# Attention heads divided before the turn instead of after it, and V's bias added to the heads

## The chip, the core and the metric

The kernel runs on one core of a Trainium2 chip. The core has five engines that each run their own instruction stream in order: TensorE (PE, its weight loads PEld), VectorE (DVE), ScalarE (ACT), GpSimd (POOL) and SyncE (SP, which only issues DMAs). They are joined by semaphores. The metric is the device time of one execution in microseconds, and the median of several runs is compared.

## What is computed

A gated block: cross-attention from 8 x 512 tokens onto 8 x 1601 context rows (16 heads of 32), with 8-bit fake quantisation ahead of both projections, then a mixture of 32 experts with a shared expert.

```python
q = _qdq(x) @ _qdq(wq).T + bq
kv = cond @ wkv.T + bkv
k, v = jnp.split(kv, 2, axis=-1)          # heads of 32
attn = jax.nn.softmax(jnp.einsum('bnhd,bmhd->bhnm', q, k) * scale, axis=-1)
o = jnp.einsum('bhnm,bmhd->bnhd', attn, v).reshape(B, N, C)
out = _qdq(o) @ _qdq(wp).T + bp
...
x = x + jnp.tanh(g_xattn[0]) * xattn(_layernorm(x), ctx_2048, ...)
x = x + jnp.tanh(g_ffn[0]) * ffn(_layernorm(x), ...)
```

The softmax weights of a token sum to one, so adding V's bias to V before the weighted sum is the same as adding it to the divided head after it.

## The kernel before

Attention goes through 8 batches `b`, in each 4 groups `g` of 4 heads, in each 13 steps `kt` of 128 context rows: 416 steps, named by `steps()`. A step on TensorE computes the scores of four heads, transposed (`scores_of`, two PSUM banks `s_ps` in turn), ScalarE takes Exp of each into `probs` (`exp_of`), and a step later TensorE adds `probs` times V to the heads `o_ps` (`heads_of`). A score matmul waits for the Exp of two heads before it. The sums of the Exps go another way: GpSimd adds ten of the thirteen steps into `prob_acc`, and TensorE multiplies that and the other three steps by ones into `sum_ps` (`sums_of`, `accumulated_sums`). Each head's sum lies there repeated over its 32 rows.

Between the score matmuls of a group stands other work, as a list of tiles that all engines read from the same functions (`lead_tiles`, `fill_tiles`), and that share four PSUM banks `r_all` in turn (`Ring`). Each tile takes the next bank, and TensorE waits until the tile four places earlier has been drained. In a step, the list is spread over the four heads by its length. For the next group these tiles are: the query tile and two of four K pieces (step 0), two more K pieces (step 1), 64 `max` tiles (steps 3 to 11), from which VectorE takes the row maxima, and their turn. ScalarE and VectorE split each K piece into two fp16 parts, SyncE copies the parts into a stack for each head (L539), and the first max tile of a head waits for those DMAs. V tiles of the next batch stand in group 3 (steps 3 to 8) and group 0 (steps 1, 2, 4, 5, 7, 8, 10). VectorE drains them and adds V's bias on the way (L1259).

When a group is over, ScalarE copies the heads (`copy_heads`, L1070) and, once GpSimd's part is in, the sums (`copy_sums`, L1075). Later TensorE turns both, tokens into rows: tile `oT` (L773, four transposes) and tile `sumT` (L778, four fp32 matmuls with every 32nd column of the identity). VectorE inverts the turned sums, 16 a row (L1309), and multiplies (L1313) into `work`. Where the turn stands: step 2 of groups 2, 3 and 0 of the next batch, and step 10 of group 1 (`LATE_HEADS`).

Row work is spread over the steps too, and stands behind a step's tiles: `o_part` in group 0 (ScalarE's rounding behind steps 4 and 5, L973, its integers behind steps 7 and 8, L980), `h_part` in group 1 (VectorE's layernorm statistics behind step 0, L1193 and L1196, ScalarE's square root inside step 1, L960), `x_part` in group 2.

Of the kernel before, what the change touches and what calls it, by code (L numbers as in the profile page):

```python
# [26 lines left out]
P = 128  # L27
# [66 lines left out]
def head_tiles(b, g):  # L94
    return [("oT", b, g), ("sumT", b, g)]
# [138 lines left out]
def build(nc, x, ctx_in, g_xattn, g_ffn, wq, bq, wkv, bkv, wp, bp, gate_w, gate_bias, w1, w2, w3,  # L234
# [15 lines left out]
    with ctx:  # L250
# [69 lines left out]
        rsum = sb("rsum", [P, TT, GH], FP32)  # L320
# [127 lines left out]
        sums_copied = sem("sums_copied")  # L448
# [212 lines left out]
        def _(pe):  # L661
# [42 lines left out]
            def tile(key):  # L704
# [64 lines left out]
                elif kind == "oT":  # L769
                    pe.wait_ge(heads_copied, group(b, key[2]) + 1)  # L770
# [3 lines left out]
                elif kind == "sumT":  # L774
                    pe.wait_ge(sums_copied, group(b, key[2]) + 1)
                    ps = open_tile(*key)
                    for t in range(TT):
                        last = nc.tensor.matmul(ps[:, t * GH:(t + 1) * GH], sum_sb[:, t * P:(t + 1) * P],  # L778
                                                ident[:, ::DH], start=True, stop=True)
# [80 lines left out]
            def sums_of(s):  # L860

                kt = s % KT
                w, slot = rows(kt), s % HALVES
                if kt == FIRST_SUMS and s >= KT:
                    pe.wait_ge(sums_copied, s // KT)
                for j in range(GH):
                    last = nc.tensor.matmul(sum_ps[j * DH:(j + 1) * DH, :], ones[0:w, :], probs[0:w, slot, j, :],
                                            start=(kt == FIRST_SUMS), stop=False)
                last.then_inc(probs_used, 1)
# [71 lines left out]
        def _(act):  # L941
# [64 lines left out]
            def tile(key):  # L1006
# [8 lines left out]
                elif kind == "k":  # L1015
                    g, i = key[2:]
                    at, w = PIECE_AT[i], PIECE[i]
                    if i == 0 and group(b, g):

                        for j in range(GH):  # L1020
# [3 lines left out]
                                         bias=bk_col[:, g:g + 1]).then_inc(k_hi_ready, 1)  # L1024
                elif kind == "maxT":
# [41 lines left out]
            def copy_heads(n):  # L1067

                act.wait_ge(probs_used, (n + 1) * KT)
                nc.scalar.copy(oT_sb[:, :], o_ps[:, :]).then_inc(heads_copied, 1)  # L1070

            def copy_sums(n):

                act.wait_ge(acc_summed, n + 1)
                nc.scalar.copy(sum_sb[:, :], sum_ps[:, :]).then_inc(sums_copied, 1)  # L1075
# [7 lines left out]
            for b, g, kt in steps():  # L1083
                s = step_of(b, g, kt)
                fill = fill_tiles(b, g, kt)
                if kt == 0 and s:
                    copy_heads(s // KT - 1)
                for key in lead_tiles(b, g, kt):
                    tile(key)
                for j in range(GH):  # L1090
                    exp_of(s, j)
                    if j == 1 and g == 2 and b + 1 < B and kt == X_STD:
                        deviations(x_var_ready, b + 2, x_std_ready)
                    if j == 1 and g == 1 and b and kt == H_STD:
                        deviations(h_var_ready, b, h_std_ready)
                    for key in fill[len(fill) * j // GH:len(fill) * (j + 1) // GH]:
                        tile(key)
                if kt == 0 and s:
                    copy_sums(s // KT - 1)
                if g == 2 and b + 1 < B:  # L1100
                    x_part(b + 1, kt)
                if g == 0 and b:
                    o_part(b - 1, kt)
                if g == 1 and b:
                    h_part(b - 1, kt)
            copy_heads(B * GROUPS - 1)
            copy_sums(B * GROUPS - 1)
# [26 lines left out]
        def _(dve):  # L1134
# [110 lines left out]
            def tile(key):  # L1245
# [9 lines left out]
                elif kind == "v":  # L1255
                    t = key[2]
                    w = rows(t)
                    ps = full(dve, *key)
                    V.tensor_tensor(v_sb[0:w, t, :], ps[0:w, :], bv_row[0:w, :], ALU.add).then_inc(free_of(*key), 1)  # L1259
# [31 lines left out]
                elif kind == "sumT":  # L1291
# [11 lines left out]
            def heads_out(b, g):  # L1303

                if g == 0 and b:
                    dve.wait_ge(h_out, b * DMA)
                po = full(dve, "oT", b, g)
                pss = full(dve, "sumT", b, g)
                V.reciprocal(rsum[:, :, :].rearrange("p t j -> p (t j)"), pss[:, 0:TT * GH]  # L1309
                             ).then_inc(free_of("sumT", b, g), 1)  # L1310
                wait_read(dve, "sumT", b, g)
                for t in range(TT):
                    last = V.tensor_tensor(  # L1313
                        work[:, t, g * P:(g + 1) * P].rearrange("p (j d) -> p j d", j=GH),
                        po[:, t * P:(t + 1) * P].rearrange("p (j d) -> p j d", j=GH),
                        rsum[:, t, :].unsqueeze(2).to_broadcast([P, GH, DH]), ALU.mult)
                    if t < TT - 1:
                        step.mark(last)
                last.then_inc(free_of("oT", b, g), 1)
                wait_read(dve, "oT", b, g)  # L1320

# [4 lines left out]
            for b, g, kt in steps():  # L1326
                for key in lead_tiles(b, g, kt) + fill_tiles(b, g, kt):
                    tile(key)
                if g == 2 and b + 1 < B:
                    x_part(b + 1, kt)  # L1330
                if g == 0 and b:
                    o_part(b - 1, kt)
                if g == 1 and b:
                    h_part(b - 1, kt)
            heads_out(B - 1, GROUPS - 1)
# [313 lines left out]
```

## Time and profile before

| | us |
|---|---|
| median of three runs | 3153.32 |
| lowest, highest | 3148.29, 3154.59 |
| the profiled execution | 3147.53 |
| its span, first to last instruction | 3145.8 |
| one batch of attention | 300 |

The profile is one execution, taken by the hardware profiler. An idle time in it is given with the instruction that ended it (`<-`). "issue" is idle time for which the profile shows nothing. A wait on a weight load (PEld) is hidden in part by the matmul still running; the wait on the matmul itself (PE) is TensorE standing still. [...] Batches 1 to 7 repeat the same pattern to a few tenths of a microsecond.

### The profile page before, as it was taken

How to read it: one execution, taken by the hardware profiler on the slowest of the kernel's cores; microseconds unless marked ns; L12 is line 12 of the kernel's file. 1: busy time of each engine (PE TensorE's matmuls, PEld its weight loads, DVE VectorE, ACT ScalarE, POOL GpSimd, SP SyncE). 2: the span in 40 equal slices, each digit the busy share in tenths (PEclk: the TensorE clock that was granted, in tenths of full speed). 3: DMA queues.
4: the chain of work that ended last, by engine and by line, in shares of the span. 5: the costliest groups of instructions: out<-in, count | busy, mean ns of one | idle time of the engine just before them, and what ended most of it. 6: DMA issues, size and time to landing. Idle time of an engine off the chain costs nothing. (4 is left out here: it accounts for less than half of the span.)

```text
span 3145.8 us, 43433 instructions
## 1 busy us (share of the span) xinstructions
PE 2824.6 (90%) x14876; PEld 1215.4 (39%) x14876; DVE 1791.0 (57%) x3878; ACT 1383.7 (44%) x2460; POOL 1808.2 (57%) x1570
## 2 busy tenths in 40 slices
PE   5898999899989988999899899989998799998987
PEld 3333333333333333333333333333332354444766
DVE  6576567756675666667557756775664343433222
ACT  4155446644564456456545644564456210000111
POOL 0285567656656676667566656765668423223455
PEclk9798999999999999999999999999999899899999
DMA  4111012101211031103111201221011123131996
GB/s 126 39 45 52 24 35 72 54 22 35 77 53 39 18 94 47 35 22 95 30 35 58 66 23 35 72 54 33 23 53 57 68 99 110 61 121 55 310 282 116
DMA packets 146586, 215.59 MB, mean 69 GB/s; under 512 B 24984, under 2 KB 78232, under 8 KB 146368
## 3 DMA queue, kind: packets, MB, share of 16 engines
q1 hardware_dynamic: 130496, 195.95, 20.7%
q0 software_dynamic: 15872, 16.87, 2.9%
q8 instruction: 120, 1.97, 0.3%
q14 instruction: 98, 0.80, 0.1%
HBM read 126.49 MB, written 34.24 MB: 51 GB/s over the span
## 5 line engine op out<-in xcount | busy, mean ns | idle before, releaser
L1549 POOL TENSOR_TENSOR prob_acc<-prob_acc,probs 128x512 f32<-128x512 f32 x1152 | 1430.7, 1279 | 420.6 <-ACT probs L1065 420.6
L1065 ACT ACTIVATE probs<-s_ps 128x512 f32<-128x512 f32 (+1 forms) x1664 | 937.2, 596 | 770.0 <-PE s_ps L841 738.8
L1286 DVE TENSOR_REDUCE piece_max<-r_all 128x1 f32<-128x400 f32 (+1 forms) x2048 | 1027.7, 565 | 142.1 <-PE r_all L763 135.3
L763 PE MATMUL r_all<-k_flat,q_stack 96*128 96x400 f16 (+1 forms) x2048 | 604.7, 352 | 110.2 <-DVE piece_max L1286 41.4
L841 PE MATMUL s_ps<-q_stack,k_flat 97*128 97x512 f16 (+1 forms) x1664 | 631.1, 396 | 60.7 <-ACT probs L1065 52.5
L855 PE MATMUL o_ps<-probs,v_sb 128*32 128x512 f32 (+1 forms) x3328 | 465.3, 632 | 21.6 <-ACT probs L1065 21.6
L841 PEld LDWEIGHTS s_ps<-q_stack,k_flat 97*128 97x128 f16 (+1 forms) x1664 | 160.1, 101 | 630.5 <-ACT probs L1065 424.5
L1546 POOL COPY prob_acc<-probs 128x512 f32<-128x512 f32 x128 | 73.0, 616 | 494.1 <-PE sum_ps L875 359.5
L763 PEld LDWEIGHTS r_all<-k_flat,q_stack 96*128 96x128 f16 x2048 | 203.7, 100 | 387.7 <-DVE piece_max L1286 125.8
L1581 POOL DMA_INDIRECT slot_rows<-payload,slot x128 | 125.7, 982 | 300.1 <-DVE slot L1462 230.7
L1280 DVE SCALAR_TENSOR_TENSOR k_lo<-r_all,bk_col,k_hi 128x400 f16<-128x400 f32 (+1 forms) x128 | 81.7, 638 | 280.7 <-ACT k_hi L1023 280.7
L810 PE MATMUL r_all<-probs,k_flat 128*128 128x512 f32 x512 | 225.6, 599 | 0.9 <-DVE sum_sb L1424 0.9
L1259 DVE TENSOR_TENSOR v_sb<-r_all,bv_row 128x512 f32<-128x512 f32 (+1 forms) x104 | 71.8, 690 | 170.4 <-PE r_all L724 170.4
L1023 ACT ACTIVATE k_hi<-r_all,bk_col 128x400 f16<-128x400 f32 (+1 forms) x128 | 76.5, 598 | 182.5 <-PE r_all L753 182.5
L1608 POOL DMA_INDIRECT out_rows<-probs,slot_init x64 | 99.8, 1559 | 87.7 <-DMA out_rows<-probs,slot_init 52.2
L810 PEld LDWEIGHTS r_all<-probs,k_flat 128*128 128x128 f32 x512 | 97.5, 192 | 120.7 <-issue 119.7
L1054 ACT ACTIVATE oT_sb<-r_all 128x512 f32<-128x512 f32 x32 | 19.1, 597 | 259.7 <-PE r_all L810 243.9
L828 PE MATMUL r_all<-k_flat,probs 128*128 128x512 f32 x256 | 130.0, 667 | 1.5 <-DVE probs L1429 0.9
L855 PEld LDWEIGHTS o_ps<-probs,v_sb 128*32 128x32 f32 (+1 forms) x3328 | 66.7, 109 | 130.4 <-issue 70.8
L724 PE MATMUL r_all<-wkv_hi,ctx_hi 128*128 128x512 f16 (+1 forms) x416 | 112.8, 395 | 3.4 <-DVE ctx_lo L1252 1.8
L753 PE MATMUL r_all<-ctx_hi,wkv_hi 128*128 128x400 f16 (+1 forms) x512 | 109.6, 336 | 0.0
L724 PE MATMUL r_all<-wkv_hi,ctx_lo 128*128 128x512 f16 (+1 forms) x416 | 108.8, 385 | 0.0
(220 smaller groups left out, 2832.3 us busy)
## 6 DMA issues: line engine op xcount, KB each, us to landing
k_flat<-k_hi SPq DMA_DIRECT2D x256, 100.1 KB, 2.2
ctx_raw<-in_ctx SPq DMA_DIRECT2D x96, 256.0 KB, 2.8
xin<-in_x SPq DMA_DIRECT2D x16, 1024.0 KB, 5.6
k_flat<-k_lo SPq DMA_DIRECT2D x128, 100.1 KB, 2.2
v_sb<-in_L_ffn_w SPq DMA_DIRECT2D x18, 512.0 KB
q_stack<-q_hi SPq DMA_DIRECT2D x256, 32.0 KB, 1.8
h_rows<-work SPq DMA_DIRECT2D x8, 1024.0 KB, 4.5
x_rows<-xin SPq DMA_DIRECT2D x8, 1024.0 KB, 6.8
```

The source lines that it names most:

```text
L724: last = nc.tensor.matmul(ps[0:w, :], a[:, c, t * P:t * P + w], wt[:, 1, c, :], start=(n == 0), stop=(n == 3 * DC - 1))
L753: last = nc.tensor.matmul(ps[:, 0:w], wt[:, 0, c, g * P:(g + 1) * P], a[:, c, at:at + w], start=(n == 0), stop=(n == 3 * DC - 1))
L763: last = nc.tensor.matmul(ps[:, 0:w], q_stack[0:KSPLIT, g % 2, j, qt * P:(qt + 1) * P], k_stack[0:KSPLIT, g % 2, j, at:at + w], start=True ...
L810: last = nc.tensor.matmul(ps[:, :], wt[:, c, f * P:(f + 1) * P], hT[:, c, :], start=(c == 0), stop=(c == DC - 1))
L828: last = nc.tensor.matmul(ps[:, :], actT[:, f, t * P:(t + 1) * P], sd[:, f, :], start=(f == 0), stop=(f == FSC - 1))
L841: nc.tensor.matmul(s_ps[j % SBANKS][0:w, :], k_stack[:, g % 2, j, kt * P:kt * P + w], q_stack[:, g % 2, j, :], start=True, stop=True).then ...
L855: last = nc.tensor.matmul(o_ps[j * DH:(j + 1) * DH, :], v_sb[0:w, kt, h * DH:(h + 1) * DH], probs[0:w, slot, j, :], start=(kt == 0), stop= ...
L1065: nc.scalar.activation(probs[0:w, slot, j, :], s_ps[j % SBANKS][0:w, :], ACT.Exp).then_inc(probs_ready, 1)
L1286: V.reduce_max(piece_max[:, j * TT + qt, i:i + 1], ps[:, 0:PIECE[i]], X_AXIS).then_inc(free_of(*key), 1)
L1549: last = G.tensor_tensor(prob_acc[:, j, :], prob_acc[:, j, :], probs[:, slot, j, :], ALU.add)
L1581: G.indirect_dma_start(out=slot_scr, out_offset=bass.IndirectOffsetOnAxis(ap=slot[:, t, k:k + 1], axis=0), in_=payload[:, t, k, :], in_off ...
L1608: G.indirect_dma_start(out=out, out_offset=bass.IndirectOffsetOnAxis(ap=e_slots[:, e, 0:1].bitcast(I32), axis=0), in_=e_y[e % 2][:, h * HA ...
```

## The change

ScalarE no longer copies the sums, and TensorE no longer turns them. Instead VectorE, behind its tiles of step 0 of the next group, waits for the sums, inverts all of `sum_ps` into `sum_sb` (128x512) and multiplies the copied heads by it in place (`divide_heads`). The turn of the heads waits for that. What is turned is then already divided: VectorE adds V's bias to it in one operation on its way into `work` (`heads_out`). V tiles leave PSUM as plain copies on ScalarE. `copy_heads` now waits for the turn of the group before, which reads the buffer it writes.

```diff
 def head_tiles(b, g):
-    return [("oT", b, g), ("sumT", b, g)]
+    return [("oT", b, g)]
...
                 elif kind == "oT":
-                    pe.wait_ge(heads_copied, group(b, key[2]) + 1)
+                    pe.wait_ge(heads_divided, group(b, key[2]) + 1)
...
-                elif kind == "sumT":
-                    pe.wait_ge(sums_copied, group(b, key[2]) + 1)
-                    ps = open_tile(*key)
-                    for t in range(TT):
-                        last = nc.tensor.matmul(ps[:, t * GH:(t + 1) * GH], sum_sb[:, t * P:(t + 1) * P],
-                                                ident[:, ::DH], start=True, stop=True)
...
                 if kt == FIRST_SUMS and s >= KT:
-                    pe.wait_ge(sums_copied, s // KT)
+                    pe.wait_ge(sums_inverted, s // KT)
...
+                elif kind == "v":
+                    t = key[2]
+                    w = rows(t)
+                    ps = full(act, *key)
+                    nc.scalar.copy(v_sb[0:w, t, :], ps[0:w, :]).then_inc(free_of(*key), 1)
...
                 act.wait_ge(probs_used, (n + 1) * KT)
+                if n:
+                    act.wait_ge(bank_full[ring.last_bank("oT", (n - 1) // GROUPS, (n - 1) % GROUPS)],
+                                ring.done("oT", (n - 1) // GROUPS, (n - 1) % GROUPS))
                 nc.scalar.copy(oT_sb[:, :], o_ps[:, :]).then_inc(heads_copied, 1)
-
-            def copy_sums(n):
-
-                act.wait_ge(acc_summed, n + 1)
-                nc.scalar.copy(sum_sb[:, :], sum_ps[:, :]).then_inc(sums_copied, 1)
...
-                    V.tensor_tensor(v_sb[0:w, t, :], ps[0:w, :], bv_row[0:w, :], ALU.add).then_inc(free_of(*key), 1)
...
-                V.reciprocal(rsum[:, :, :].rearrange("p t j -> p (t j)"), pss[:, 0:TT * GH]
-                             ).then_inc(free_of("sumT", b, g), 1)
...
+                V.tensor_tensor(work[:, :, g * P:(g + 1) * P], po[:, :].rearrange("p (t n) -> p t n", t=TT),
+                                bv_row[:, g * P:(g + 1) * P].unsqueeze(1).to_broadcast([P, TT, P]), ALU.add
+                                ).then_inc(free_of("oT", b, g), 1)
                 wait_read(dve, "oT", b, g)
+
+            def divide_heads(n):
+
+                dve.wait_ge(acc_summed, n + 1)
+                V.reciprocal(sum_sb[:, :], sum_ps[:, :]).then_inc(sums_inverted, 1)
+                dve.wait_ge(sums_inverted, n + 1)
+                dve.wait_ge(heads_copied, n + 1)
+                V.tensor_tensor(oT_sb[:, :], oT_sb[:, :], sum_sb[:, :], ALU.mult).then_inc(heads_divided, 1)
...
+                if kt == 0 and s:
+                    divide_heads(s // KT - 1)
                 if g == 2 and b + 1 < B:
                     x_part(b + 1, kt)
```

The order on the engines shows three places; `r_all` is the shared PSUM, `probs` the Exps, `x4` four instructions in a row. First VectorE at the start of group 1 of batch 1, before:

```order
L1280 SCALAR_TENSOR_TENSOR k_lo<-r_all,bk_col,k_hi 128x401
L1280 SCALAR_TENSOR_TENSOR k_lo<-r_all,bk_col,k_hi 128x400
L1193 BN_STATS stats<-xin 128x6 x4
L1196 BN_AGGR mv<-stats 128x2 x4
L1280 SCALAR_TENSOR_TENSOR k_lo<-r_all,bk_col,k_hi 128x400 x2
```

and the same place now:

```order
L1269 SCALAR_TENSOR_TENSOR k_lo<-r_all,bk_col,k_hi 128x401
L1269 SCALAR_TENSOR_TENSOR k_lo<-r_all,bk_col,k_hi 128x400
L1305 RECIPROCAL sum_sb<-sum_ps 128x512
L1308 TENSOR_TENSOR oT_sb<-oT_sb,sum_sb 128x512
L1187 BN_STATS stats<-xin 128x6 x4
L1190 BN_AGGR mv<-stats 128x2 x4
L1269 SCALAR_TENSOR_TENSOR k_lo<-r_all,bk_col,k_hi 128x400 x2
```

The reciprocal and the product stand ahead of the statistics and of K's pieces 2 and 3. Next ScalarE in group 0 of batch 1, steps 1 to 8, before:

```order
L1023 ACTIVATE k_hi<-r_all,bk_col 128x400
L1065 ACTIVATE probs<-s_ps 128x512 x13
L973 ACTIVATE work<-work,rounder,inv 128x512 x2
L1065 ACTIVATE probs<-s_ps 128x512 x4
L973 ACTIVATE work<-work,rounder,inv 128x512 x2
L1065 ACTIVATE probs<-s_ps 128x512 x8
L980 ACTIVATE q_int<-work,rounder 128x512 x2
```

and now:

```order
L1064 ACTIVATE probs<-s_ps 128x512 x10
L1023 COPY v_sb<-r_all 128x512
L967 ACTIVATE work<-work,rounder,inv 128x512 x2
L1064 ACTIVATE probs<-s_ps 128x512 x4
L1023 COPY v_sb<-r_all 128x512
L967 ACTIVATE work<-work,rounder,inv 128x512 x2
L1064 ACTIVATE probs<-s_ps 128x512 x8
L1023 COPY v_sb<-r_all 128x512
L974 ACTIVATE q_int<-work,rounder 128x512 x2
```

A copy of V stands directly ahead of each pair of rounding and integer operations. Last TensorE in group 1 of batch 0, at the turn behind step 10's max tiles, before:

```order
L773 MATMUL r_all<-ident,oT_sb 128x128 x4
L778 MATMUL r_all<-ident,sum_sb 128x4 x4
L841 MATMUL s_ps<-q_stack,k_flat 128x512
L763 MATMUL r_all<-k_flat,q_stack 128x401
L763 MATMUL r_all<-k_flat,q_stack 128x400
```

and now:

```order
L773 MATMUL r_all<-ident,oT_sb 128x128 x4
L835 MATMUL s_ps<-q_stack,k_flat 128x512
L763 MATMUL r_all<-k_flat,q_stack 128x401
L763 MATMUL r_all<-k_flat,q_stack 128x400
```

The four matmuls of the sum tile are gone from between the turn and the next step.

## Rows read from the trace of the kernel before

**Rows 1.** The page, part 1: busy us (share of span), instructions, by engine

```profile
PE 2824.6 (90%) x14876; PEld 1215.4 (39%) x14876; DVE 1791.0 (57%) x3878; ACT 1383.7 (44%) x2460; POOL 1808.2 (57%) x1570
```

**Rows 2.** Line L763, the max tiles: whom TensorE waited for, us, times

```profile
  DVE work L1313: 24.0, 30
...
  DVE v_sb L1259: 14.7, 51
```

**Rows 3.** Groups by line: operation, shapes, count | busy us, mean ns | idle before

```profile
L1070 ACT COPY oT_sb<-o_ps 128x512 f32<-128x512 f32 x32 | 18.8, 586 | 65.1 <-PE sum_ps L867 65.1
...
L1309 DVE RECIPROCAL rsum<-r_all 128x16 f32<-128x16 f32 x32 | 8.0, 250 | 92.1 <-PE r_all L778 92.1
...
L1144 DVE RECIPROCAL inv<-so 128x4 f32<-128x4 f32 x8 | 1.4, 178 | 0.3
L1462 DVE TENSOR_TENSOR slot<-slotf,over 128x16 int32<-128x16 f32 x8 | 1.4, 175 | 0.3
```

**Rows 4.** Timeline, batch 4, group 0, steps 2 and 3: start, duration, instruction [idle before]

```profile
1325.98 1.08 PEld L778 LDWEIGHTS r_all<-ident,sum_sb 128*128 128x128 f32 x8
...
1327.55 0.88 DVE L1313 TENSOR_TENSOR work<-r_all,rsum 128x128 f32<-128x128 f32 x4
...
1328.48 0.34 PE L763 MATMUL r_all<-k_flat,q_stack 96*128 96x400 f16 x1 [0.54 <-DVE work L1313]
```

**Rows 5.** Timeline, step 3 of group 3 (batch 3) and of group 2 (batch 4)

```profile
1250.63 0.52 PE L763 MATMUL r_all<-k_flat,q_stack 96*128 96x401 f16 x2 [1.34 <-DMA k_flat<-k_hi]
...
1470.31 0.61 PE L841 MATMUL s_ps<-q_stack,k_flat 97*128 97x512 f16 x1 [2.31 <-ACT probs L1065]
```

**Rows 6.** Timeline, batch 4, group 0, around the ends of steps 4 and 7

```profile
1337.77 1.51 ACT L973 ACTIVATE work<-work,rounder,inv 128x512 f32<-128x512 f32 x2
...
1341.70 0.69 DVE L1259 TENSOR_TENSOR v_sb<-r_all,bv_row 128x512 f32<-128x512 f32 x1 [2.81 <-PE r_all L724]
...
1341.99 1.14 ACT L1065 ACTIVATE probs<-s_ps 128x512 f32<-128x512 f32 x2 [2.72 <-PE s_ps L841]
...
1343.71 0.10 PEld L841 LDWEIGHTS s_ps<-q_stack,k_flat 97*128 97x128 f16 x1 [0.84 <-ACT probs L1065]
...
1357.08 1.32 ACT L980 ACTIVATE q_int<-work,rounder 128x512 bf16<-128x512 f32 x2
...
1359.83 0.69 DVE L1259 TENSOR_TENSOR v_sb<-r_all,bv_row 128x512 f32<-128x512 f32 x1 [1.49 <-PE r_all L724]
...
1361.84 0.10 PEld L841 LDWEIGHTS s_ps<-q_stack,k_flat 97*128 97x128 f16 x1 [0.84 <-ACT probs L1065]
```

**Rows 7.** Timeline, VectorE at K's piece 2, step 1 of batch 3's group 3

```profile
1242.96 0.64 DVE L1280 SCALAR_TENSOR_TENSOR k_lo<-r_all,bk_col,k_hi 128x400 f16<-128x400 f32 x1 [4.99 <-ACT k_hi L1023]
```

**Rows 8.** Timeline, batch 4, group 1, steps 0 to 3

```profile
1395.47 2.46 DVE L1193 BATCH_NORM_STATS2 stats<-xin 128x6 f32<-128x512 f32 x4
...
1397.37 0.59 ACT L1075 COPY sum_sb<-sum_ps 128x512 f32<-128x512 f32 x1 [0.37 <-PE sum_ps L875]
...
1397.97 0.38 DVE L1196 BATCH_NORM_AGGREGATE mv<-stats 128x2 f32<-128x6 f32 x4
...
1400.25 0.30 ACT L960 ACTIVATE std<-mv,eps 128x4 f32<-128x4 f32 x1
...
1403.22 0.10 PEld L841 LDWEIGHTS s_ps<-q_stack,k_flat 97*128 97x128 f16 x1 [0.17 <-ACT probs L1065]
...
1408.29 0.34 PE L763 MATMUL r_all<-k_flat,q_stack 96*128 96x401 f16 x1 [1.80 <-DMA k_flat<-k_hi]
```

**Rows 9.** Windows: us; busy of PE, PEld, DVE, ACT, POOL; clock; DMA share, GB/s

```profile
1408.30:1412.30 4.00, 4.00 (x16) 0.96 (x17) 1.63 (x3) 0.72 (x2) 4.00 (x4) 0.57 0.67 156
```

**Rows 10.** Timeline, the end of attention

```profile
2457.04 1.12 PE L773 MATMUL r_all<-ident,oT_sb 128*128 128x128 f32 x4
...
2457.17 0.59 ACT L1075 COPY sum_sb<-sum_ps 128x512 f32<-128x512 f32 x1 [7.64 <-PE sum_ps L875]
...
2459.54 3.65 PE L797 MATMUL r_all<-ident,ctx_lo 128*128 128x128 f32 x16
```

More of the change, by code:

```diff
@@ L319, in build @@
         prob_acc = sb("prob_acc", [P, GH, N], FP32)
-        rsum = sb("rsum", [P, TT, GH], FP32)
         hT, actT = probs[:, 0], probs[:, 1]
@@ L447, in build @@
         heads_copied = sem("heads_copied")
-        sums_copied = sem("sums_copied")
+        sums_inverted = sem("sums_inverted")
+        heads_divided = sem("heads_divided")
         h_ready = sem("h_ready")
@@ L1097, in _ @@
                         tile(key)
-                if kt == 0 and s:
-                    copy_sums(s // KT - 1)
                 if g == 2 and b + 1 < B:
@@ L1106, in _ @@
             copy_heads(B * GROUPS - 1)
-            copy_sums(B * GROUPS - 1)
             for key in [("hT", 0, c) for c in range(DC)] + [("logits", 0)]:
@@ L1254, in tile @@
                                     ctx_hi[:, :, t * P:t * P + w], ALU.subtract).then_inc(free_of(*key), 1)
[L1255 to L1258, printed above, removed]
-                    V.tensor_tensor(v_sb[0:w, t, :], ps[0:w, :], bv_row[0:w, :], ALU.add).then_inc(free_of(*key), 1)
                 elif kind == "q":
@@ L1290, in tile @@
                         V.reduce_max(row_max[:, :], piece_max[:, :, :], X_AXIS).then_inc(row_max_ready, 1)
-                elif kind == "sumT":
+                elif kind == "oT":
                     heads_out(b, key[2])
@@ L1307, in heads_out @@
                 po = full(dve, "oT", b, g)
-                pss = full(dve, "sumT", b, g)
-                V.reciprocal(rsum[:, :, :].rearrange("p t j -> p (t j)"), pss[:, 0:TT * GH]
-                             ).then_inc(free_of("sumT", b, g), 1)
[L1311 to L1319, printed above, removed]
-                wait_read(dve, "oT", b, g)
+                V.tensor_tensor(work[:, :, g * P:(g + 1) * P], po[:, :].rearrange("p (t n) -> p t n", t=TT),
+                                bv_row[:, g * P:(g + 1) * P].unsqueeze(1).to_broadcast([P, TT, P]), ALU.add
+                                ).then_inc(free_of("oT", b, g), 1)
+                wait_read(dve, "oT", b, g)
+            def divide_heads(n):
[4 more added lines that the diff above has]
+                V.tensor_tensor(oT_sb[:, :], oT_sb[:, :], sum_sb[:, :], ALU.mult).then_inc(heads_divided, 1)
             for key in first_tiles():
@@ L1326, in _ @@
             for b, g, kt in steps():
+                s = step_of(b, g, kt)
                 for key in lead_tiles(b, g, kt) + fill_tiles(b, g, kt):
                     tile(key)
+                if kt == 0 and s:
+                    divide_heads(s // KT - 1)
                 if g == 2 and b + 1 < B:
@@ L1334, in _ @@
                     h_part(b - 1, kt)
+            divide_heads(B * GROUPS - 1)
             heads_out(B - 1, GROUPS - 1)
```

## The prediction

> **What bounds the kernel now.** I read the page first: TensorE is busy for 90% of the span, VectorE and GpSimd for 57%, ScalarE for 44% [rows 1]. A change elsewhere moves the end only if it moves a moment at which TensorE starts something. So I next read whom TensorE waits for ahead of its max tiles (L763): for the head tile's drain on VectorE (L1313) 24.0 us, for the V tile's drain on VectorE (L1259) 14.7 us [rows 2]. The 24.0 us count each wait twice, once for the weight load and once for the matmul, so 30 entries are 15 places. The durations come from the view by lines [rows 3], and the places from the timeline of one batch, which repeats every 300 us.
>
> **The sum tile goes away.** Its four fp32 matmuls keep TensorE's queue for 1.08 us [rows 4], and the head tile ahead of it is drained only once both are turned: the max tile that needs its bank stood still for 0.54 us more. There are 32 head tiles, and they stand in five kinds of place.
> - In group 0 at step 2 (7 batches) and in group 1 at step 10 (8 batches) nothing else waits: these are the 15 places above. Of 1.08 us about 0.95 is time that nothing else used, and with 0.54 us the gain is 1.5 us each, 15 x 1.5 = 22 us. The drain itself falls from 0.25 + 0.88 us [rows 3, 4] to one 128x512 addition, 0.69 us [rows 6], so I expect no wait in its place.
> - In group 2 at step 2 (8 places) TensorE waits 2.31 us for the Exp behind the square root, and in group 3 at step 2 (8 places) 1.34 us for the K stack [rows 5]. The wait grows by what the sum tile leaves: gain 0. If that cover went, each would be worth 1 us.
> - At the end of attention (1 place) it is counted below.
>
> **V leaves PSUM by ScalarE.** 104 tiles move. VectorE's add of 0.69 us ends the wait of 14.7 us, a copy takes 0.586 us [rows 2, 3, 6], so a bank comes free 0.1 us earlier: 51 waits x 0.1 = 5 us, with 0 and 14.7 as bounds. On ScalarE the copy stands behind the step's last Exp and ahead of the next step's first. In group 3 that time is idle. In group 0 it is not: at steps 4, 5, 7 and 8 ScalarE rounds the quantised heads (1.51 us) or turns them into integers (1.32 us), and did so while TensorE computed V. Now these instructions are queued behind a copy that waits for V to be complete. At step 4, V is complete at 1341.70; copy 0.59, rounding 1.51: the first Exp of step 5 starts at 1343.8 instead of 1341.99 and ends at 1344.4, and the third score matmul, which ran at 1343.71, waits for it: 0.75 us. At step 7: complete 1359.83, + 0.59 + 1.32 = 1361.75, Exp to 1362.35, against a score matmul at 1361.84: 0.55 us [rows 6]. Step 8 gives 0.1 by the same working, step 5 nothing, since the sum matmuls over step 4 lie between. That is 1.4 us x 7 batches = 10 us lost; the bounds are 5 (half of it finds slack) and 20 (0.75 at each of four steps).
>
> **The division ahead of the turn.** VectorE now waits for the group's sums, inverts 128x512 from PSUM, and multiplies 128x512. The trace has no reciprocal of this size. A reciprocal of 4 columns takes 178 ns and one of 16 takes 250 ns: 6.0 ns a column, so 512 columns take 0.178 + 508 x 0.0060 = 3.2 us. An addition takes 175 ns for 16 columns [rows 3] and 0.69 us for 512 [rows 6], 1.04 ns a column. Bounds: 0.69 us, if a long reciprocal streams like the addition and the 250 ns are a short instruction's overhead, and 6.2 us, if half of the 12 columns between the two hid in it (12 ns a column). I take 3.2, as the two rows are the same instruction, and 2.5 to 4.2 as near it. [...]
>
> Where does the wait stand? At step 0 of each group, ahead of K's pieces 2 and 3 on VectorE. In groups 0, 2 and 3 VectorE was idle for 4.99 us there [rows 7]; with 3.2 + 0.7 us K's piece 2 is drained about 1 us late and piece 3, which starts the stack's DMAs, on time. That costs nothing as long as the reciprocal is under 5 us.
>
> In group 1 (7 batches) the statistics of the next layernorm (2.46 + 0.38 us) stood in that idle time and were done before the sums came. Now they are queued behind the division, and ScalarE's square root, in the middle of step 1, waits for them, and with it K's piece 2, the Exp table and all later Exps. From [rows 8]: sums complete 1397.37, + 3.2 + 0.07 (semaphore) + 0.69 + 0.07, then 2.88 for the statistics: 1404.3, against the square root at 1400.25. The delay is R + 0.83 with R the reciprocal, so 4.0 us. TensorE has no slack there: its first score matmul of step 2 already waited 0.17 us for an Exp, and K's piece 3 on ScalarE comes after those Exps, so the DMA that TensorE awaits at 1408.29 moves by the same 4.0 us. 7 x 4.0 = 28 us lost.
>
> A second price there is the clock. [...] Another wait of 4 us comes now. [...] I take 0 and keep 12 for the range.
>
> **The end of attention.** The turn of the last heads went ahead at 2457.04, without the sums; now it waits for the division, from 2457.17 to 2461.2, then takes 1.1 us, and the 16 transposes of the next stage, at 2459.54 [rows 10], start at 2462.3: 2.8 us lost. The first stage and everything past it don't change.
>
> **Sum:** -22 - 5 + 10 + 28 + 2.8 = +14 us. The profiled execution took 3147.5 us (span 3145.8 and 1.7 around it) and would take 3161; the median of the three runs is 5.8 us above it, and from there I predict 3167 us, 0.4% slower than that median.
>
> **Rivals.**
> 1. The reciprocal streams. R = 0.69: group 1 loses 7 x 1.5 = 10.6 us, the end 0.3, and the sum is -22 - 5 + 10 + 10.6 + 0.3 = -6, 3147 us: faster. It decides from R under 1.5 us, where the sum crosses zero (8R - 12). Against it: six adds' worth a column in both short ones. For it: only short ones are seen, and a short instruction's fixed part may hold it all. [...] 0.12.
> 2. The clock falls a second time in group 1 after the longer wait: +12 on my sum, 3179 us. For it: one short wait did it. Against: the two waits are parted by work, and a slow stretch between them hides in the second. 0.14.
> 3. The change takes the sum tile from TensorE but the gain doesn't arrive, as the turned tile, now one place later in its step, is waited for as before: +22, 3189 us. Against it: nothing but VectorE's drain was late there, and it gets shorter. 0.06.
> 4. ScalarE's and group 1's delays are partly made up by slack that I don't see (half of 38 us): -5, 3148 us. Against it: TensorE's waits there end on exactly these rows. 0.09.
> 5. The reciprocal takes over 5 us. At 6.2 group 1 loses 21 more, the end 3, and K's piece 3 is 1.2 us late in the other 24 places, 29 us: +67, 3220 us. For it: nothing longer than 16 columns was seen. Against it: the two rows. 0.05.
>
> **How the numbers follow.** My case holds 0.54, from 3157 to 3180 by R from 2.5 to 4.2 and the bounds on V. A measurement of this kernel tells 0.2% (6.3 us) from no change. Range: from 3149, which leaves out most of rival 1, to 3184, which takes in rival 2. Faster 0.11 (most of rival 1), same 0.18 (rival 4, the rest of 1, and the low edge of my case), slower 0.71.
>
> **What would show it.** Right: the reciprocal of 128x512 near 3.2 us; the square root in group 1 four microseconds later behind the statistics, with TensorE idle for them at step 2; the wait on L1313's successor near 0; the Exp after rounding in group 0 at 1.8 us later, with a wait of the third score matmul. Wrong: a reciprocal near 0.7 us or over 5 us (then K's piece 3 is late in every group), or waits for the head tile's division ahead of the turn.

## The result and the profile after

| | before | changed |
|---|---|---|
| median of six runs, us | 3150.81 | 3177.34 |
| lowest, highest, us | 3142.89, 3158.37 | 3167.34, 3180.49 |
| profiled execution (span), us | 3147.53 (3145.8) | 3177.9 (3176.1) |

The ratio is 1.008 (95% interval 1.0059 to 1.0102): slower, as forecast and within the range, but by 26.5 us where the sum said 14. That is four times the 0.2% that the prediction took as the least that can be told.

The page of the changed kernel, part 1 (answers [rows 1]) and two groups of part 5, the new reciprocal and V's copies (operation, shapes, count | busy us, mean ns | idle before):

```profile
PE 2814.8 (89%) x14580; PEld 1192.5 (38%) x14620; DVE 1856.0 (58%) x3710; ACT 1419.9 (45%) x2532; POOL 1823.7 (57%) x1570
...
L1305 DVE RECIPROCAL sum_sb<-sum_ps 128x512 f32<-128x512 f32 x32 | 107.5, 3358 | 105.0 <-PE sum_ps L869 105.0
...
L1023 ACT COPY v_sb<-r_all 128x512 f32<-128x512 f32 (+1 forms) x104 | 61.0, 586 | 223.4 <-PE r_all L724 223.4
```

TensorE has 10 us less to do, and the profiled execution takes 30 us longer. The reciprocal takes 3.36 us. Whom the max tiles of L763 waited for, with the weight loads, us and times, in the changed kernel (answers [rows 2]):

```profile
  ACT v_sb L1023: 9.3, 51
  DVE work L1297: 6.1, 16
```

The two waits that the change was to shorten are shorter: 24.0 us became 6.1, and 14.7 became 9.3. What grew is seen in the view of waits on TensorE itself (us in total, times, longest us), for the score matmuls and the K stack. Before:

```profile
PE s_ps L841 <- ACT probs L1065: 52.5, 66, 2.3
...
PE r_all L763 <- DMA k_flat<-k_hi: 34.1, 17, 3.4
```

The same two rows in the changed kernel:

```profile
PE s_ps L835 <- ACT probs L1064: 89.2, 85, 3.7
...
PE r_all L763 <- DMA k_flat<-k_hi: 24.7, 17, 3.6
```

36.7 us more for Exps, 9.4 us less for the K stack. The timeline of batch 4, group 1, shows where (answers [rows 8]; start, duration, instruction [idle before]):

```profile
1400.83 1.06 PE L869 MATMUL sum_ps<-prob_acc,ones 128*32 128x512 f32 x8
...
1401.96 3.36 DVE L1305 RECIPROCAL sum_sb<-sum_ps 128x512 f32<-128x512 f32 x1 [1.81 <-PE sum_ps L869]
...
1405.36 0.84 DVE L1308 TENSOR_TENSOR oT_sb<-oT_sb,sum_sb 128x512 f32<-128x512 f32 x1
...
1406.12 2.46 DVE L1187 BATCH_NORM_STATS2 stats<-xin 128x6 f32<-128x512 f32 x4
...
1409.03 0.30 ACT L954 ACTIVATE std<-mv,eps 128x4 f32<-128x4 f32 x1 [4.30 <-DVE mv L1190]
...
1411.78 1.10 PE L835 MATMUL s_ps<-q_stack,k_flat 97*128 97x512 f16 x2 [3.73 <-ACT probs L1064]
...
1416.84 0.34 PE L763 MATMUL r_all<-k_flat,q_stack 96*128 96x401 f16 x1 [0.50 <-DMA k_flat<-k_hi]
```

The square root stood still for 4.30 us behind the statistics, TensorE for 3.73 us behind the Exps. From the accumulated sums to the first max tile it is 1416.84 - 1400.83 = 16.01 us; before it was 12.06 (its sums start at 1396.23, the max tile at 1408.29 [rows 8]).

The end of attention, timeline of the changed kernel (answers [rows 10]):

```profile
2471.68 1.94 PE L869 MATMUL sum_ps<-prob_acc,ones 128*32 128x512 f32 x8 [6.30 <-POOL prob_acc L1541]
...
2477.89 1.11 PE L773 MATMUL r_all<-ident,oT_sb 128*128 128x128 f32 x4 [4.28 <-DVE oT_sb L1308]
...
2478.80 3.62 PE L791 MATMUL r_all<-ident,ctx_lo 128*128 128x128 f32 x16
...
2483.30 7.01 PE L798 MATMUL r_all<-gateT,probs 128*128 128x32 f32 x32 [0.88 <-ACT probs L1040]
```

Sums to transposes: 7.12 us, 4.37 before, and 7.01 us for 32 router matmuls that took 4.62 before.

**The stages.** The window from the first accumulated sums to the last, before (us; busy of PE, PEld, DVE, ACT, POOL; TensorE's granted clock as a share of full speed; DMA share, GB/s):

```profile
198.60:2455.17 2256.57, 2053.71 (x11527) 778.76 (x11526) 1429.69 (x2815) 1229.98 (x2184) 1490.08 (x1269) 0.96 0.17 47
```

And in the changed kernel:

```profile
198.71:2471.68 2272.97, 2037.62 (x11243) 748.95 (x11279) 1499.41 (x2662) 1259.60 (x2244) 1506.07 (x1269) 0.95 0.17 47
```

Attention takes 16.4 us more. Divided at each start of accumulated sums, the seven spans of group 0 take 6.3 us more in all, the eight of group 1 10.3 more, group 2 0.9 less, group 3 0.8 more. The router stage behind it (up to the first bias of the shared expert) takes 22.1 us instead of 17.0. That is 21.5 us in the stages that the change touches. Another 9 us of the two traces' difference lie in the shared expert, whose code is the same. Its window before:

```profile
2472.18:2920.70 448.52, 412.63 (x1292) 209.73 (x1291) 171.61 (x717) 48.46 (x85) 132.99 (x146) 0.91 0.26 86
```

and after:

```profile
2493.80:2951.80 458.00, 420.56 (x1291) 216.32 (x1291) 171.64 (x717) 48.58 (x85) 132.50 (x146) 0.90 0.25 84
```

The same matmuls were busy 8 us longer at a slightly lower granted clock (0.90 against 0.91). In these traces the clock is at one of two levels: in windows of half a microsecond over batch 4's group 1 of before it is 1.00 up to 1408.5 us, 0.50 from 1409.0 to 1411.5 and 1.00 again from 1412.0 on.

### The profile page after: what moved, and what is told of

It reads as the page before. It is cut to its first block and busy times, and to the rows that moved or that the text cites. A ratio compares the mean times of both kernels' runs of the same rounds, so it can differ in the third digit from the quotient of the medians.

```text
span 3176.1 us, 42792 instructions
## 1 busy us (share of the span) xinstructions
PE 2814.8 (89%) x14580; PEld 1192.5 (38%) x14620; DVE 1856.0 (58%) x3710; ACT 1419.9 (45%) x2532; POOL 1823.7 (57%) x1570
## 5 line engine op out<-in xcount | busy, mean ns | idle before, releaser
L1541 POOL TENSOR_TENSOR prob_acc<-prob_acc,probs 128x512 f32<-128x512 f32 x1152 | 1446.6, 1290 | 435.6 <-ACT probs L1064 435.5
L763 PE MATMUL r_all<-k_flat,q_stack 96*128 96x400 f16 (+1 forms) x2048 | 604.6, 352 | 95.8 <-DVE piece_max L1275 45.2
L763 PEld LDWEIGHTS r_all<-k_flat,q_stack 96*128 96x128 f16 x2048 | 204.2, 100 | 369.0 <-DVE piece_max L1275 130.1
L1305 DVE RECIPROCAL sum_sb<-sum_ps 128x512 f32<-128x512 f32 x32 | 107.5, 3358 | 105.0 <-PE sum_ps L869 105.0
L1023 ACT COPY v_sb<-r_all 128x512 f32<-128x512 f32 (+1 forms) x104 | 61.0, 586 | 223.4 <-PE r_all L724 223.4
```

What stands on the lines that cost most here:

```text
L763: last = nc.tensor.matmul(ps[:, 0:w], q_stack[0:KSPLIT, g % 2, j, qt * P:(qt + 1) * P], k_stack[0:KSPLIT, g % 2, j, at:at + w], start=True ...
L1305: V.reciprocal(sum_sb[:, :], sum_ps[:, :]).then_inc(sums_inverted, 1)
L1541: last = G.tensor_tensor(prob_acc[:, j, :], prob_acc[:, j, :], probs[:, slot, j, :], ALU.add)
```

## The experiments

They ran in three sets (e1 to e4, e5 to e8, e9 and e10) on three chips, where the kernel before has medians of 3099.3, 3098.8 and 3098.7 us instead of 3151, so evidently not on the chip of the pair above. Ratios are compared, each to the runs of before in its own set, and traces of these runs with each other. First the pair once more. "Before again" is the kernel before, "after again" the changed kernel.

> The kernel before once more, for a second trace. The stretch after attention is within 3 us of the first trace's if the clock's phase there is fixed by the program; if it is chance, it differs by as much as the two traces of the changed kernel do.

> The changed kernel once more, for a second trace. If the stretch after attention, which the change does not touch, really got longer, it is again 9 to 13 us longer than in the trace of before; if that is the clock's phase in one execution, it differs from the first trace by several us.

The results of all, with the attention (first accumulated sums to last) and the router stage of the profiled execution, and the mean length of group 0 and 1 in batches 1 to 6:

| kernel | ratio to before (95%) | attention | router | group 0 | group 1 |
|---|---|---|---|---|---|
| before again | 1 | 2257.5 | 17.0 | 84.6 | 61.2 |
| after again | 1.0074 (1.0050 to 1.0098) | 2276.0 | 19.9 | 85.2 | 62.4 |
| e1, statistics first | 0.9996 (0.9973 to 1.0019) | 2247.4 | 19.4 | 85.0 | 58.5 |
| e2, V copies only | 1.0016 (1.0000 to 1.0033) | 2246.6 | 17.2 | 85.8 | 59.7 |
| e3, division only | 1.0042 (1.0029 to 1.0056) | 2262.4 | 20.0 | 83.5 | 63.6 |
| e5, rows ahead of V | 1.0075 (1.0050 to 1.0099) | 2273.5 | 20.0 | 83.4 | 63.6 |
| e6, turn behind transposes | 1.0088 (1.0060 to 1.0116) | 2274.1 | 15.4 | 84.9 | 62.7 |
| e7, e1 + e5 + e6 | 0.9944 (0.9923 to 0.9965) | 2230.0 | 13.9 | 83.5 | 59.3 |
| e9, e1 + e5 | 0.9950 (0.9927 to 0.9973) | 2230.7 | 19.9 | 83.2 | 59.4 |
| e10, e3 + e1 + e6 | 0.9918 (0.9894 to 0.9943) | 2237.2 | 13.9 | 83.2 | 59.7 |

The pair repeats: attention and router stage together are 21.4 us longer here (18.5 + 2.9), 21.5 on the first chip. Place by place they differ: group 0 is 5.6 us longer (6.3 on the first chip), group 1 7.0 (10.3), and groups 2 and 3 together 6.0, which on the first chip were 0.1 shorter. The shared expert's stage is 4 us shorter after than before, with the clock at 0.97 and 0.98, and what follows it 6 us longer (228.1 against 221.8, on the first chip 224.3 against 225.1). The code of both is the same, so nothing shows that the 9 us in the first pair of traces come from the change. Group 0 of the changed kernel swings alike on both chips: 86.6 to 86.7, 84.8, 84.8, 83.3 to 83.4, 88.0, 83.4, 86.7 for batches 1 to 7, where before it held within 0.7 us. It swings with the granted clock. Windows over the group in batches 1, 3 and 4, changed kernel, first chip (columns as in [rows 9]):

```profile
410.21:496.95 86.74, 80.06 (x425) 29.79 (x426) 54.88 (x91) 43.10 (x78) 53.28 (x44) 0.96 0.08 20
...
1015.25:1100.07 84.82, 78.19 (x425) 29.32 (x426) 54.88 (x91) 43.09 (x78) 53.28 (x44) 0.98 0.08 20
...
1317.47:1400.83 83.36, 76.67 (x424) 28.94 (x425) 54.88 (x91) 42.81 (x78) 53.30 (x44) 1.00 0.09 20
```

The two groups of 83.4 us have 1.00, the two of 84.8 have 0.98, and the three of 86.7 and more have 0.96. All groups 0 of before have 0.98. Batch 5, the longest, has 1.2 us more besides, at one place in its last third that these runs leave unexplained.

### e1: the statistics of group 1 ahead of the division

```diff
+                if g == 1 and b:
+                    h_part(b - 1, kt)
                 if kt == 0 and s:
                     divide_heads(s // KT - 1)
...
-                if g == 1 and b:
-                    h_part(b - 1, kt)
```

> The changed kernel, but in group 1 VectorE runs the layernorm statistics ahead of the division, as it ran them ahead of the sums before. Theory 1 (the statistics queued behind the division hold ScalarE's square root, and TensorE 3.7 us, in 7 batches): the wait of the step-2 score matmul in group 1 is back near 0.2 us, each group 1 of batches 1 to 7 is 2 to 4 us shorter than in the changed kernel (61.8 to 63.8 us there, sums to sums), so 59 us, a little under the 60.5 of before for the missing sum tile; in all 15 to 28 us under the changed kernel, 3150 to 3162 us. Rival (V's copies and the clock carry the loss): within 5 us of the changed kernel, 3172 or more.

The ratio falls from 1.0074 to 0.9996, some 24 us and within the 15 to 28 expected, and the attention by 28.7. Batch 4, group 1, timeline of e1:

```profile
1393.17 1.06 PE L869 MATMUL sum_ps<-prob_acc,ones 128*32 128x512 f32 x8
...
1395.20 3.33 DVE L1305 RECIPROCAL sum_sb<-sum_ps 128x512 f32<-128x512 f32 x1
...
1397.08 0.30 ACT L954 ACTIVATE std<-mv,eps 128x4 f32<-128x4 f32 x1
...
1405.22 0.34 PE L763 MATMUL r_all<-k_flat,q_stack 96*128 96x401 f16 x1 [1.79 <-DMA k_flat<-k_hi]
```

The reciprocal takes as long as ever (3.33 us against 3.36), but stands behind the statistics. The square root waits for nothing, and from sums to max tile it is 12.05 us, the 12.06 of before. So the price of group 1 was not the reciprocal but what was queued behind it.

### e2 and e3: each half alone

e2 is the kernel before with V drained by copies on ScalarE; V's bias is left out of its computation. e3 is the changed kernel with V drained and biased by VectorE as before, and the turned heads only copied.

```diff
+                    nc.scalar.copy(v_sb[0:w, t, :], ps[0:w, :]).then_inc(free_of(*key), 1)
...
-                    V.tensor_tensor(v_sb[0:w, t, :], ps[0:w, :], bv_row[0:w, :], ALU.add).then_inc(free_of(*key), 1)
```

> The kernel before, but ScalarE copies V out of PSUM; V's bias is left out of the computation altogether. Sum tile, division and turn are as before. Theory 1 (a copy ahead of ScalarE's rounding and integers in group 0 delays the next Exps): group 0 of batches 1 to 7 about 1.4 us longer (84.5 before), group 3 unchanged, 5 to 10 us over before in all, 3156 to 3161 us. Rival (VectorE relieved of 0.69 us per V tile, banks free earlier): 5 to 10 us under before.

> The changed kernel, but VectorE drains V with its bias added, as before, and the turned heads are only copied into the rows. Theory 1: the division alone costs 28 us in group 1 and 5 at the end, its missing sum tile gives 22 back and the clock some: 5 to 15 us over before, and with the V copies' part the measured 26 of the whole. Rival (division harmless, V's move carries the loss): within 3 us of before or faster.

By medians V's copies cost 5 us (by the interval hardly to be told from none), the division 13 to 15, the two 18 to 20 of the 23 to 26 of the whole. V's copies make group 0 1.2 us longer, with the clock at 0.98 in all batches as before. The division makes it 1.1 us shorter, and 0.8 in the six batches that are at 0.98 (83.7 against 84.5 and 84.6): that is the sum tile's gain. Each half alone is steady, e3 at 83.6 to 83.9 in six batches of seven, e2 at 85.7 to 86.0 in all, so the swings of the changed kernel come with neither half alone, but only with both. The profiled execution of e2 is 13 us under its own median and has an attention shorter than before, by group 1: a place in which e2 changes nothing. What differs there is the clock. The 4 us after the wait for the K stack in batch 4, group 1, in windows of before again:

```profile
1411.16:1415.16 4.00, 3.93 (x15) 0.92 (x16) 1.63 (x3) 0.63 (x2) 4.00 (x4) 0.57 0.68 158
```

and of e2:

```profile
1407.11:1411.11 4.00, 3.95 (x22) 1.28 (x22) 3.05 (x7) 2.22 (x4) 4.00 (x4) 1.00 0.67 158
```

The same wait of 1.8 us, the same instructions, and TensorE gets through 15 matmuls at 0.57 and through 22 at 1.00.

### e5: ScalarE's row work ahead of V's copy

```diff
-                        tile(key)
+                        if not (key[0] == "v" and g == 0 and kt in O_ROUND + O_INT):
+                            tile(key)
...
                     o_part(b - 1, kt)
+                    for key in fill:
+                        if key[0] == "v" and kt in O_ROUND + O_INT:
+                            tile(key)
```

> The changed kernel, but at steps 4, 5, 7 and 8 of group 0 ScalarE does the rounding and the integers ahead of the copy of V, in the time in which TensorE computes V. Theory 1: the wait of the third score matmul behind these steps goes, 1.4 us per batch: 5 to 12 us under the changed kernel, which is 0.74% over before: a ratio to before of 1.003 to 1.006. Rival (V's copies cost nothing there): 1.007 or more.

Timeline of batch 5, group 0, the end of step 4, in the changed kernel (ScalarE's rows and the score matmul behind them):

```profile
1644.39 0.59 ACT L1023 COPY v_sb<-r_all 128x512 f32<-128x512 f32 x1 [4.27 <-PE r_all L724]
...
1644.88 1.52 ACT L967 ACTIVATE work<-work,rounder,inv 128x512 f32<-128x512 f32 x2
...
1646.30 2.28 ACT L1064 ACTIVATE probs<-s_ps 128x512 f32<-128x512 f32 x4
...
1646.93 0.39 PE L835 MATMUL s_ps<-q_stack,k_flat 97*128 97x512 f16 x1 [0.46 <-ACT probs L1064]
```

and the same place in e5:

```profile
1647.62 0.58 ACT L1023 COPY v_sb<-r_all 128x512 f32<-128x512 f32 x1 [2.66 <-PE r_all L724]
...
1648.10 1.10 ACT L1064 ACTIVATE probs<-s_ps 128x512 f32<-128x512 f32 x2
...
1649.64 0.39 PE L835 MATMUL s_ps<-q_stack,k_flat 97*128 97x512 f16 x1
```

From V's copy to the score matmul it is 2.54 us in the changed kernel and 2.02 in e5: 0.52 us at step 4. The same two rows at step 7 are 2.36 us apart (1665.21 and 1667.57), so 0.35. At step 8 it is 0.07. And at step 5, where the prediction saw nothing, 0.49 is lost another way: VectorE's clipping of the rounded heads (L1207, L1211 in e5) takes 2.51 us instead of 2.02, and the max tile behind it waits the longer. Batch 4, the changed kernel:

```profile
1360.00 0.73 PE L763 MATMUL r_all<-k_flat,q_stack 96*128 96x401 f16 x2 [1.34 <-DVE piece_max L1275]
```

and e5:

```profile
1358.18 0.74 PE L763 MATMUL r_all<-k_flat,q_stack 96*128 96x401 f16 x2 [0.84 <-DVE piece_max L1279]
```

Why the clipping takes longer there is not shown. The four places make 1.43 us, which is the whole difference where the clock is the same: in batch 4 it is 1.00 over group 0 in both kernels, and the group takes 83.36 us in the changed kernel and 81.93 in e5:

```profile
1316.68:1398.61 81.93, 76.69 (x426) 28.97 (x426) 54.75 (x91) 42.90 (x78) 53.14 (x44) 1.00 0.09 21
```

So the mechanism is as predicted, and group 0 falls by 1.75 us to 83.4 in the mean (five batches of seven at 83.4 to 83.6). Yet the ratio stays at 1.0075, where 1.003 to 1.006 was expected and 1.007 or more stood for V's copies costing nothing. By the ratio alone that rival would stand; the trace rules it out, and shows where the gain went: group 1, untouched by the edit, takes 63.6 us instead of 62.4. Windows of batch 4's group 1, from 8 us behind the start of the sums on, in the changed kernel:

```profile
1408.83:1412.83 4.00, 1.05 (x6) 0.24 (x6) 0.90 (x5) 3.77 (x7) 1.03 (x1) 0.86 0.00 0
1412.83:1416.83 4.00, 3.04 (x12) 0.40 (x11) 1.44 (x3) 2.29 (x5) 4.00 (x5) 0.71 0.43 99
1416.83:1420.83 4.00, 3.99 (x22) 1.27 (x22) 3.09 (x7) 2.50 (x5) 4.00 (x4) 1.00 0.68 158
```

and in e5:

```profile
1406.61:1410.61 4.00, 0.97 (x6) 0.35 (x10) 0.90 (x5) 3.79 (x7) 1.05 (x1) 1.00 0.00 0
1410.61:1414.61 4.00, 2.81 (x12) 0.25 (x4) 1.44 (x3) 2.50 (x5) 4.00 (x5) 0.53 0.44 99
1414.61:1418.61 4.00, 4.00 (x14) 0.91 (x15) 1.63 (x3) 0.60 (x1) 4.00 (x4) 0.50 0.68 157
```

After the same long wait the changed kernel has its low stretch while TensorE waits for the K stack, and is at 1.00 when the max tiles restart (22 matmuls in 4 us). In e5 the low stretch begins later and lies on the restart (14 matmuls). This batch is e5's worst (66.0 us against 61.8), the other five take 61.7 to 63.8 against 61.8 to 63.8. It goes so in all batches: in the four groups 1 of 61.8 to 61.9 us of the changed kernel the clock in the 4 us from the first max tile on is 1.00, in the three of 63.3 to 63.8 it is 0.50 to 0.59, and in e3 it is 0.50 to 0.61 in all seven, which take 63.3 to 64.3. What shifts it is not shown, only that it goes with the work ahead.

### e6: the last turn behind the next stage's transposes

```diff
-            for key in head_tiles(B - 1, GROUPS - 1) + [("hT", 0, c) for c in range(DC)] + [("logits", 0)]:
+            for key in [("hT", 0, c) for c in range(DC)] + head_tiles(B - 1, GROUPS - 1) + [("logits", 0)]:
```

> The changed kernel, but at the end of attention TensorE turns the first rows of the next stage ahead of the divided heads instead of behind them. Theory 1: the 4.3 us in which TensorE waits for the division are filled, the first router scores come some 5 us earlier (2.8 us of wait and 2.4 us of matmuls at the lower clock), and the ratio is 0.0010 to 0.0025 under the changed kernel's 1.0074 or, by its own uncertainty, not to be told from it; the trace tells. Rival (the slower start there is the clock's own): the router's 32 matmuls take 7 us again.

The end of attention in the timeline of e6:

```profile
2476.32 3.52 PE L791 MATMUL r_all<-ident,ctx_lo 128*128 128x128 f32 x16
...
2480.67 0.66 PE L773 MATMUL r_all<-ident,oT_sb 128*128 128x128 f32 x4 [0.82 <-DVE oT_sb L1308]
...
2481.16 5.22 PE L798 MATMUL r_all<-gateT,probs 128*128 128x32 f32 x32
```

The wait of 4.28 us is 0.82, and the router stage takes 15.4 us instead of 19.9. What is gained is the wait: the 32 router matmuls take 5.22 us, and 5.03 in after again, so the 7.01 of the first chip were not there to be won back. 4.5 us are under 0.2% of the kernel, and the ratio, 1.0088, can't be told from 1.0074.

### e7, e9 and e10: together

> Statistics ahead of the division, row work ahead of V's copies and the turn behind the next stage's transposes, all three. By Theory 1 all the losses are gone and the sum tile's 22 us and the banks' 5 are left: 25 to 40 us under the changed kernel, so a ratio to before of 0.990 to 0.997. Rival (the gains of the sum tile are themselves taken up by TensorE's clock or by waits that follow): 0.998 to 1.002, as the statistics alone gave 0.9996.

> The changed kernel with the statistics of group 1 ahead of the division and with ScalarE's rounding and integers ahead of the V copy in group 0; the last turn is left where the change has it. If the parts add (the row work ahead of V is worth about 1.75 us a batch in group 0 once group 1 has no long wait, 12 us, and the turn behind the transposes 4.5 us), the attention takes about 2230 us as in the kernel with all three, the router stage 20 us instead of 14, and the ratio is 0.9955 to 0.9965. If the gain of all three hung on the turn at the end, or the clock takes back what group 0 gives as it did without the statistics' move, the ratio is 0.999 to 1.000, that of the statistics' move alone.

> The division ahead of the turn with the statistics ahead of it in group 1 and the last turn behind the next stage's transposes, but V leaves PSUM by VectorE with its bias, and the turned heads are only copied. No V copy stands on ScalarE here, so its row work needs no move. If all the gain comes from the sum tile that is gone, group 0 takes 83.4 us and the ratio is that of the kernel with all three, 0.994 to 0.996. If V on ScalarE has a worth of its own (a bank 0.1 us earlier, and in group 1 the granted clock, which stayed at 1.00 only in kernels that had V's copies on ScalarE), group 1 takes 60 us or more here instead of 59.0 and the ratio is 0.997 to 0.999.

All three are faster than the kernel before, by 0.5 to 0.8%, and so than the changed one. e7 is where it was expected, e9 a little and e10 clearly lower. The attention window of e7:

```profile
199.16:2429.15 2229.99, 2026.57 (x11279) 746.08 (x11279) 1499.33 (x2662) 1259.20 (x2244) 1500.87 (x1269) 0.96 0.17 48
```

and of e10:

```profile
199.05:2436.23 2237.18, 2033.74 (x11279) 753.58 (x11278) 1543.11 (x2753) 1214.14 (x2153) 1499.65 (x1269) 0.96 0.17 48
```

Without the long wait in group 1, e5's edit keeps its gain in group 0: e7 and e9 have 83.2 to 83.5 there. Not all of the rest is of its making. Against e1, e9 is 12 us shorter in the seven groups 0 and 6 us longer in the eight groups 1 (59.4 against 58.5 in the mean, as the low stretch is back at the restart of the max tiles, with 0.50 to 0.68 over 4 us in six batches of seven where e1 has 0.57 in two and 1.00 in five), and 11 us shorter in groups 2 and 3, which the edit doesn't touch. e9 against e7 says that the last turn's 6 us (13.9 against 19.9 in the router stage) are too few to show in the ratio, and that the gain doesn't hang on them. e10 leaves V where it was. Whom its max tiles wait for:

```profile
  DVE v_sb L1248: 14.7, 51
```

That is the wait of [rows 2] again, and the kernel is no slower for it: the intervals of 0.9944, 0.9950 and 0.9918 touch or overlap, and the last is the lowest. Its attention is 7 us longer than e7's in the profiled executions, 4 of them in group 3, and the medians don't show them. Nor is the 60 us in group 1 reached that would have spoken for a worth of V on ScalarE (59.7 in the mean, 59.2 to 59.4 in five batches of six). So that half of the change has no gain of its own that the times can tell. What e7 to e10 gain is in the main the sum tile, once nothing is lost for it. Their groups 0 and 1 are together 22 to 25 us shorter than in before again. Of that the clock has a part: (1 - clock) x 2 x length, added up over these groups, is 45 to 49 us at the lower level (0.50) instead of 61, worth 6 to 8 us at half speed. Some 16 to 17 us are left, an estimate, as not all of the low time is work.

## Why the prediction was right in sign and short in size

- **The sum tile goes away (-22).** The waits went as said ([rows 2] 24.0 to 6.1), but the gain is smaller than the 1.5 us a place of the sum. At the same clock it is 0.8 us in group 0 (e3 above) and 1.1 in group 1: e10 takes 59.2 to 59.4 us where before takes 60.5, both with the low stretch at the restart (0.57 to 0.64 over 4 us, and 0.57 to 0.60). 7 x 0.8 + 8 x 1.1 = 14 us, and 16 to 17 by the totals of e7 to e10. In groups 2 and 3 it was to be 0. On the first chip they sum to the same 1177 us as before within 0.2, in e3 they are 1.6 us shorter than in before again, in after again 6.0 longer. So 0 fits, within what the clock moves there.
- **V's bank earlier (-5).** The wait fell by 5.4 us, right as a wait, but it was hardly one of TensorE's own. The 14.7 us of [rows 2] count the weight loads with the matmuls. The view of waits on TensorE itself has, before, a single one for V's drain:

```profile
PE r_all L763 <- DVE v_sb L1259: 0.3, 1, 0.3
```

The rest lay on the weight loads, hidden behind the matmul still running; the prediction allowed for this with the head tile and not here. At a clock of 0.98, e5's group 0 is 0.2 to 0.3 us shorter than e3's, 2 us in seven batches. By its time e10, which hasn't it, isn't slower: on the whole it was worth nothing that can be told.
- **ScalarE's row work (+10).** Right in size, 1.43 us a batch at the same clock against 1.4, and right in mechanism at three of the four steps (e5). It is made up otherwise: 0.53, 0.49, 0.34 and 0.07 us at steps 4, 5, 7 and 8 instead of 0.75, 0, 0.55 and 0.1. The sum added the durations on ScalarE end to end, while in the rows each starts 0.10 us ahead of the end of the one before (copy 1644.39 + 0.59, rounding at 1644.88). And step 5 loses through VectorE's clipping, which the prediction left out. That two errors cancel is luck.
- **Group 1 (+28).** The reciprocal took 3.36 us against 3.2, and 3.95 us against 4.0 were lost up to the max tiles. e1 gives the same from the other side: with the order changed, the delay is zero. The eight groups 1 nevertheless grew by 10.3 us only, where -12 + 28 = 16 stood in the sum, and 19 with the sum tile at its measured worth. The clock of [rows 9] was set at no change; it paid 8 back instead, as in four batches of seven (61.8 us instead of 63.3 to 63.8) the low stretch moved from the restart of the max tiles into the wait.
- **Rival 2** (a second low stretch in group 1) came true in the other three. Over group 1 the clock is 0.92, 0.95 and 0.92 in batches 1, 5 and 7, where it is 0.97 in the other four and in most batches of before, but so much of it lies in the wait that it cost under 1 us each. In e3 all seven are at 0.92 to 0.95. No run shows the 12 us kept for this, seven times (1 - 0.57) x 4 us by [rows 9].
- **The end of attention (+2.8).** +2.75 us to the transposes. Behind them the router matmuls took 2.4 us more on the first chip, at the lower clock for the whole stage (15 us at 0.50 against 0.64 before). In the later pair they took 0.4 more (5.03 against 4.64), and the stage was 2.9 us longer in all.
- **Rivals 1 and 5** fell with the row of the reciprocal. For 512 columns it takes 6.56 ns a column, hardly more than the 6.0 between the two short ones, and nothing like the 0.69 us of an addition of that size. No run shows the 4.2 us up to which my case went: all 32 took 3.36.
- **Rival 3** (the gain doesn't arrive) is ruled out by e3 and e7.
- **Rival 4** (unseen slack) isn't there: from sums to max tile it is 16.0 us in all seven groups 1, 12.05 before but for batch 3 (13.7), and group 0 lost its 1.43 us in full.

**Three steps of the sum were off**, though the forecast held. The sum tile was put at 22 us and measured 14 to 17. V's bank was put at 5, of a wait that stood still for 0.3. And the clock was priced as a term of group 1 alone, and there at 0, while it moved every place. In the stages touched, 21.5 us were measured against +14. By place:

| | my terms | first chip | later pair |
|---|---|---|---|
| group 0 | -0.5, less a part of V's -5 | +6.3 | +5.6 |
| group 1 | +16 | +10.3 | +7.0 |
| groups 2 and 3 | 0, less a part of V's -5 | -0.1 | +6.0 |
| end of attention, router stage | +2.8 | +5.1 | +2.9 |

On the first chip group 0 adds up: -6 for the sum tile, -2 for V's bank, +10 for ScalarE's row work and +4 for the clock and batch 5's 1.2 us, as against 84.8 us at 0.98 batches 1 and 7 lost 1.9 each and batch 5 3.2, and batches 4 and 6 gained 1.5 each. In group 1 it is -9 + 28 - 8. At the end the clock took 2.4. So the sum missed group 0 by 7 us, and the luck of group 1, whose clock gave back more than the sum tile fell short by, hid it. The 6 us of groups 2 and 3 in the later pair are not explained. The remaining 5 of the 26.5 us by medians lie in no stage that the change touches; on the first chip they go with the shared expert's clock. In the later runs the traces differ by 24 us, 21 of them in the stages touched, and the times by 23 (ratio) to 26 (medians).

## What to carry to other kernels

When an instruction is put into an engine's queue, price what stands behind it and not only the instruction: 3.4 us of reciprocal cost nothing in three groups of four (in e3 group 0 is 1.1 us shorter than before, and groups 2 and 3 together are no longer) and all of their length in the fourth, and exchanging it with the statistics gave 24 us back. Where work is moved to a less busy engine, look at what else is issued in the same step there: V's copy, harmless by its busy time, stood ahead of 1.5 us of row work and ahead of the next Exp. A gain on TensorE that has been shown in one place can be spent elsewhere by the granted clock, so test the repairs together too: e5's edit alone gave nothing in the ratio, and on top of e1's it gave 14 us (0.9996 to 0.9950). The same holds for reading a trace: compare a group's length only at the same clock (group 0 of the changed kernel takes 83.4 us at 1.00 and 86.7 at 0.96).

## What the hardware showed beside this

After one and the same wait of 1.8 us in group 1 the granted clock was 0.57 for 4 us in the kernel before and 1.00 in e1 and e2 (batch 4), in e2 with the same instructions around it. Where such a stretch falls goes with the work ahead here (e5's edit stands in group 0, and the clock at the restart in group 1 is 0.50 to 0.56 in six batches of seven, where three of seven are at 0.50 to 0.59 in the changed kernel), repeats from one chip to another (group 0 of the changed kernel, batch by batch: 83.3 and 83.4 us in batch 4, 88.0 and 88.0 in batch 5), and moves single groups by 1 to 4 us. Runs of one kernel differ by more than that: e1's twelve lie between 3085.5 and 3117.4 us. And the same shared-expert code took 448 us at a clock of 0.91 on one chip (before) and 404 us at 0.97 on another (before again).

A fp32 reciprocal of 128x512 from PSUM took 3.36 us, where an addition of that size (L1259 of before) took 0.69. Next to such lengths a product of two SBUF operands is not fixed either: 0.69 us at the end of attention, 0.84 us in group 1, and 1.20 us in e1's batch 4.
